# A sort that runs beside two-layer experts: one stage in place of two, the experts' pace over all of it, and the sorted keys stored by GpSimd's queue

## The reference, cut to what matters

```
src = concatenate([edge_index[0], loops]);  dst = concatenate([edge_index[1], loops])
ee    = exp(e - e_max[dst]);  alpha = ee / (segment_sum(ee, dst)[dst] + 1e-16)
agg   = segment_sum(h[src] * alpha, dst) + b_gat          # per token, 16 numbers
scores = layernorm(agg).reshape(M, HEADS, 4).mean(1)      # top 2 of 4 experts, softmax
for ei in range(4):
    hh  = gelu(x @ W1[ei] + b1[ei])                       # 128 -> 256
    out = out + g[..., None] * (hh @ W2[ei] + b2[ei])     # 256 -> 128
```

## Time and profile before

| what | us |
|---|---|
| three timed runs | 8943.16, 8943.4, 8950.78 |
| the profiled execution, its own time | 8939.67 |
| its span | 8937.9 |
| PE busy / DVE busy / ACT busy / POOL busy | 3473.0 / 3842.3 / 1988.6 / 5388.0 |
| mixer | 0 to 956 |
| words (first block of the sort) | 956 to 1043 |
| sort beside the experts | 1043 to 2043 |
| last merges, and the small part to its store | 2043 to 2155 |
| reading back of the keys, then the attention's first gathers | 2159 to 2207 |
| attention, then the weighing | 2207 to 8938 |

### The profile page before, as it was taken

The page is one execution under the profiler, slowest core; times in us unless marked ns, Lnnn a source line. Parts: engine busy times, 40 slices in busy tenths (PEclk is TensorE's granted clock), DMA queues, the critical chain, the costliest instruction groups (busy, mean ns, idle before and its releaser), DMA issues. The chain is left out here.

```text
span 8937.9 us, 45998 instructions
## 1 busy us (share of the span) xinstructions
PE 3473.0 (39%) x9579; PEld 1626.4 (18%) x9579; DVE 3842.3 (43%) x7346; ACT 1988.6 (22%) x3855; POOL 5388.0 (60%) x4840
## 2 busy tenths in 40 slices
PE   7888498991012222222222222222223222222134
PEld 4565244440000111011110110111101010100001
DVE  7888798788331212121212121212121212144498
ACT  6777255551011111111111110101010101001011
POOL 4555000001777777777777777777777777777452
PEclk8888699995555656656656656565666565656555
DMA  3343222220111111111111111111111111111166
GB/s 105 120 125 115 70 96 75 82 86 33 18 43 33 42 35 42 35 42 34 42 35 37 39 37 40 37 40 37 40 36 41 36 41 35 41 32 37 44 222 205
DMA packets 344241, 532.42 MB, mean 60 GB/s; under 512 B 159307, under 2 KB 236026, under 8 KB 319098
## 3 DMA queue, kind: packets, MB, share of 16 engines
q1 hardware_dynamic: 196514, 473.73, 15.2%
q0 software_dynamic: 147552, 56.95, 5.5%
HBM read 299.88 MB, written 230.45 MB: 59 GB/s over the span
## 5 line engine op out<-in xcount | busy, mean ns | idle before, releaser
L1136 POOL DMA_INDIRECT e_got<-rows,e_index x4352 | 4629.0, 1064 | 1456.0 <-issue 1456.0
L1594 PE MATMUL ex_y_ps<-ex_hh,w_w 128*128 128x512 f32 x1024 | 934.3, 1067 | 4143.2 <-issue 2577.9
L1629 DVE SCALAR_TENSOR_TENSOR ex_z<-ex_y_ps,w_b,ex_gate 128x512 f32<-128x512 f32 x192 | 144.1, 751 | 3256.4 <-remote 1924.9
L1594 PEld LDWEIGHTS ex_y_ps<-ex_hh,w_w 128*128 128x128 f32 x1024 | 295.9, 318 | 4624.3 <-issue 4115.9
L1612 ACT ACTIVATE ex_hh<-ex_hid_ps,w_b 128x512 f32<-128x512 f32 x512 | 322.5, 684 | 2550.3 <-remote 1756.6
L1126 POOL DMA_INDIRECT e_head<-rows,p_first x1 | 1.2, 1177 | 1194.1 <-issue 1194.1
L1576 PE MATMUL ex_hid_ps<-ex_tn,w_w 128*128 128x512 f32 x1024 | 639.6, 759 | 92.8 <-DMA ex_tn<-norm 67.9
L493 PE MATMUL o_hid_ps<-o_tn,w_w 128*128 128x512 f32 x1024 | 524.2, 594 | 72.0 <-DMA o_tn<-norm 72.0
L1232 DVE TENSOR_TENSOR_SCAN e_out<-e_near,e_out,e_wgt 128x64 f32<-128x64 f32 x1088 | 335.5, 364 | 459.5 <-issue 452.1
L506 PE MATMUL o_y_ps<-o_hh,w_w 128*128 128x512 f32 x1024 | 524.4, 594 | 14.7 <-ACT o_hh L524 14.7
L524 ACT ACTIVATE o_hh<-o_hid_ps,w_b 128x512 f32<-128x512 f32 x512 | 351.0, 687 | 364.8 <-PE o_hid_ps L493 364.8
(11 more groups left out here) (365 smaller groups left out, 6010.3 us busy)
## 6 DMA issues: line engine op xcount, KB each, us to landing
e_got<-rows,e_index POOLq DMA_INDIRECT x4352
kept<-o_kept SPq DMA_DIRECT2D x64, 1024.0 KB, 4.5
ex_gate<-gate SPq DMA_DIRECT2D x64, 1024.0 KB
c_kept<-kept SPq DMA_DIRECT2D x64, 1024.0 KB
sums<-e_out SPq DMA_DIRECT2D x68, 768.0 KB
m_xin<-in_x_dram SPq DMA_DIRECT2D x64, 512.0 KB, 4.6
mid<-m_xm SPq DMA_DIRECT2D x64, 512.0 KB, 2.9
norm<-m_tn SPq DMA_DIRECT2D x64, 512.0 KB, 4.9
```

Of the source, the lines that this page charges most:

```text
L1136: pool.indirect_dma_start(got[:, at % 2, c, :], None, rows_d, bass.IndirectOffsetOnAxis(ap=index[:, at % 2, c:c+1], axis=0)).then_inc(S["g ...
L1594: last = pe.matmul(self.y_ps[:, :], self.weights.w2[:, e, f, :], self.hh[:, e % 2 * HID + f, :], start=(f == 0), stop=(f == HID - 1))
```

## The change

`sort_keys` becomes one block. The tiles `src`, `dst`, `word` live as long as the rest of it. The last merges move into the generators `sorting()`, `copying()` and `turning()`, so they are units of the pace too: 474 units instead of 429. The experts' first five rounds (`EARLY`) are put ahead of all transposes and copies, with no pace; the other 60 rounds (480 gaps) are spread over the 474 units. The four transfers of sorted keys move from SP's queue to GpSimd's, on semaphores of their own.

```
-    STEPS, GAPS, AHEAD = EXPERTS * HID, EXPERTS * HID, 3
+    STEPS, GAPS, AHEAD, EARLY = EXPERTS * HID, EXPERTS * HID, 3, 5
...
-        UNITS = COL_BITS * (COL_BITS + 1) + PART_BITS * (1 + 2 * (PAIRS + 1) + PART_BITS - 1 + 2 * (COL_BITS - 1))
+        UNITS = (COL_BITS * (COL_BITS + 1) + PART_BITS * (1 + 2 * (PAIRS + 1) + PART_BITS - 1 + 2 * (COL_BITS - 1))
+                 + 1 + 2 * (PAIRS + 1) + 2 * (PART_BITS - 1) + 2 * (COL_BITS - 1))
...
+            yield None
+            yield from crossing(CROSS - 2)
+            for s in range(PART_BITS - 1):
+                yield None
+                yield None
+            yield from crossing(CROSS - 1)
+            for s in range(COL_BITS - 1):
+                yield None
+                yield None
...
-            sp.wait_ge(spent, 1)
-            sp.dma_start(high_flat.rearrange("(p f) -> p f", f=EDGE_COLS), upper[P - HALF // EDGE_COLS:P, :]).then_inc(stored, 16)
-            sp.wait_ge(stored, 48)
-            sp.dma_start(u_a[:, :], high_flat.rearrange("(p f) -> p f", p=P)).then_inc(u_back, 16)
-            sp.wait_ge(spent, 2)
-            sp.dma_start(low_rows, final_low[0][:, :]).then_inc(stored, 16)
-            sp.wait_ge(spent, 3)
-            sp.dma_start(high_flat.rearrange("(p f) -> p f", p=P), final_high[0][:, :]).then_inc(stored, 16)
...
+            pool.wait_ge(spent, 1)
+            pool.dma_start(high_flat.rearrange("(p f) -> p f", f=EDGE_COLS), upper[P - HALF // EDGE_COLS:P, :]).then_inc(away, 16)
+            pool.wait_ge(away, 16)
+            pool.dma_start(u_a[:, :], high_flat.rearrange("(p f) -> p f", p=P)).then_inc(u_back, 16)
+            pool.wait_ge(spent, 2)
+            pool.dma_start(low_rows, final_low[0][:, :]).then_inc(away, 16)
+            pool.wait_ge(spent, 3)
+            pool.dma_start(high_flat.rearrange("(p f) -> p f", p=P), final_high[0][:, :]).then_inc(away, 16)
+            pool.wait_ge(away, 48)
...
             if other:
-                pace = Pace(turning_on, UNITS, other.ROUNDS * other.GAPS)
-                for r in range(other.ROUNDS):
+                other.start_tensor(pe)
+                for r in range(other.EARLY):
+                    other.tensor(pe, r, lambda: None)
+                pace = Pace(turning_on, UNITS, (other.ROUNDS - other.EARLY) * other.GAPS)
+                for r in range(other.EARLY, other.ROUNDS):
                     other.tensor(pe, r, pace)
```

More of the change, by code:

```diff
@@ L539, in __call__, with sort_keys @@
             self.given += 1
-def sort_keys(nc, edges_d, keys_d, half, flag, other):
+def sort_keys(nc, edges_d, keys_d, half, flag, gathers, other):
     PAIRS, CELL, RING = 4, 512, 4
@@ L564, in halves @@
             return v[:, :, 0, :], (v[:, :, 1, ::-1] if mirrored else v[:, :, 1, :])
[L566 to L659, removed]
@@ L661, in sort_keys @@
+        src, dst, word = (sb(n, [P, EDGE_COLS], I32) for n in ("src", "dst", "word"))
+        if other: other.preparing(ctx)
         spans = []
@@ L713, in _ @@
         def _(sp):
+            sp.dma_start(src[:, :], edge_rows[0]).then_inc(loaded, 16)
+            sp.dma_start(dst[:, :], edge_rows[1]).then_inc(loaded, 16)
+            if other: other.start_sync(sp)
+            sp.wait_ge(const, 1)
+            sp.dma_start(keys_d[0:1].rearrange("(a b) -> a b", a=1), pad[0:1, 0:1]).then_inc(stored, 16)
+            sp.dma_start(keys_d[1 + EDGES + HALF:1 + EDGES + HALF + TAIL].rearrange("(a b) -> a b", a=P), pad[:, :]).then_inc(stored, 16)
             if other:
@@ new lines, in _ @@
+            v.wait_ge(loaded, 32)
+            if flag is not None:
+                go(v.tensor_reduce(top[:, :], dst[:, :], AX.X, ALU.max)); settle()
+                v.sem_inc(flagged, 1)
+            words(ping[:, :])
+            v.sem_inc(iota, 1)
+            if other: other.start_vector(v)
+            if flag is not None:
+                v.wait_ge(flagged, 2)
+                go(v.tensor_reduce(topf[:, :], turned_ps[0:1, 0, 0:P], AX.X, ALU.max)); settle()
+                go(v.tensor_scalar(flag, topf[:, :], float(HALF), None, ALU.is_ge)); settle()
@@ new lines, in _ @@
+            v.wait_ge(iota, 2)
+            if half:
+                go(v.tensor_scalar(pong[:, :], dst[:, :], HALF - 0.5, 16.0, ALU.subtract, ALU.mult))
+                go(v.tensor_scalar(src[:, :], dst[:, :], float(HALF), 2.0 * HALF - 1, ALU.add, ALU.min)); settle()
+                go(v.tensor_copy(dst[:, :], src[:, :])); settle()
+                words(upper[:, :])
+                go(v.tensor_tensor(upper[:, :], upper[:, :], pong[:, :], ALU.max)); settle()
+            else:
+                go(v.tensor_copy(src[:, :], dst[:, :])); settle()
+                words(upper[:, :])
@@ L785, in sorting @@
                         a, b = b, a
+                settle()
+                go(v.tensor_tensor(b[:, :], a[:, :], upper[:, :], ALU.min))
+                go(v.tensor_tensor(upper[:, :], a[:, :], upper[:, :], ALU.max)); settle()
+                v.sem_inc(spent, 1)
+                yield
+                a, b = b, a
+                yield from cross(a, b)
+                a, b = b, a
+                for s in range(PART_BITS - 1, 0, -1):
+                    yield from step(a, b, 1 << (s - 1))
+                    a, b = b, a
+                yield from cross(a, b)
+                a, b = b, a
+                for s in range(COL_BITS - 1, 0, -1):
+                    yield from step(a, b, 1 << (s - 1))
+                    a, b = b, a
                 final[:] = [a, b]
@@ L857, in _ @@
                 pass
-            for x in range(CROSS - 2, CROSS):
-                for c in range(CHUNK):
-                    copy(x, c)
             for x in range(2):
@@ L1862, in program @@
         with ExitStack() as c0:
-            sort_keys(nc, edges, keys[0], 0, flag[:, :], Outputs(nc, c0, weights, norm, kept, TOKEN_TILES))
+            sort_keys(nc, edges, keys[0], 0, flag[:, :], gathers, Outputs(nc, c0, weights, norm, kept, TOKEN_TILES))
         low = Places(nc, ctx, 0)
```

79 lines of the change are left out of this document (52 added, 27 removed).

## The result

The changed kernel takes 8900.1 us (median of five runs, 8889.7 to 8906.0), beside 8943.4 for the kernel before on the same chip (8940.9 to 8950.8). The ratio is 0.9947, with a 95% interval of 0.9936 to 0.9959: 43 us saved, 0.5%, and the interval leaves no change out. Forecast were 8895 and 8880 to 8912.

What follows compares the result with a forecast made beforehand. It took TensorE's expert rows between crossings as the sort's bound. 28.0 + 29.2 - 8.0 - 0.5 + 0.5 - 0.7 = 48.5 us off the median 8943.4 gave 8895, range 8880 to 8912.

Steps and rivals of the forecast that it cites:

- TensorE is the bound from crossing 0 on, at 0.858 us a row: In the sort from 1400 to 2043, VectorE waits for TensorE's expert rows: 0.858 us each, plus 5.67 us a crossing.
- The rival of no effect (ScalarE): Crossing waits come from ScalarE, not TensorE, so taking rows out brings nothing: 8943 us; chance 0.03.
- The slow rival: With experts spread thinner, the clock stays at 1.2 GHz for them too: about 9280 us; chance 0.04.
- Even crossings, 28.0 us: At crossings 2 to 12, fewer rows make VectorE the bound; its waits fall from 35.1 to 7.1 us.
- Odd crossings, 29.2 us: At crossings 1 to 13, TensorE stays the bound; 34 rows taken out gain 0.858 us each.
- The cold clock, -8.0: TensorE's new waits leave transposes cold at six even crossings, losing 1.34 us each; bounds 0 and 12.2.
- Crossings 14 and 15, -0.5: Lengths up to both unchanged; cold crossing 14 now costs 1.1 us, warm crossing 15 gives back 0.6.
- One block, 0.5: VectorE's 0.54 us wait at the end of the first block goes: 0.5 us gained.
- The early rounds cost nothing: The 80 early rows, 68.7 us, lie beside the making of words in TensorE's idle time, at no cost.
- GpSimd's stores, -0.7: Sorted-key stores after the sort: GpSimd's longer issue loses 0.7 us; lower end 0, upper end 8.
- The slow end of 8 us: Stores at the rate of GpSimd's small packets lose 8 us; part of the longer-tail rival, 8899 to 8907, chance 0.09.
- the smallest gain: Lower bound of the forecast's gain, given as 36 us: six crossings losing 2.03 each and stores at 8 us.

Runs made afterwards that it cites:

- early0: The changed kernel with no early rounds (EARLY 0), all 65 rounds of experts spread over the 474 units; 8901.8 us, ratio 0.9954.
- sortpace: The changed kernel, five early rounds kept, the other 60 spread over the sort's own 429 units, none beside the last merges; 8908.5 us, ratio 0.9961.
- light1: The changed kernel with a crossing counted as one unit of the pace instead of five (410 units) and one early round; 8856.7 us, ratio 0.9908.
- spstore: The changed kernel with the four transfers of sorted keys back on SP's queue; 8895.7 us, ratio 0.9946.
- light5: The changed kernel with a crossing counted as one unit of the pace, five early rounds kept; 8877.8 us, ratio 0.9917.
- light1sp: The changed kernel with crossings counted as one unit, one early round and the four sorted-key transfers on SP's queue; 8864.7 us, ratio 0.9905.
- poolonly: The kernel before with only the four transfers of sorted keys moved to GpSimd's queue; 8951.6 us against 8952.1, ratio 1.0001.
- actlight: The changed kernel with ScalarE's Gelu over 128 of its 512 columns, so the experts' outputs differ; one run, 8896.0 us.

## Why the prediction was right

The stretch explains the time in each kernel that was timed against the kernel before: 44.7 us in the stretch and 43 measured for the change, 44.8 and 40 for early0, 37.7 and 33 for sortpace, 86.8 and 85 for light1, 44.5 and 46 for spstore, 78.3 and 74 for light5, 87.1 and 87 for light1sp, -0.1 and 0.5 for poolonly.

- *TensorE is the bound from crossing 0 on, at 0.858 us a row.* Right: the model gives 19.72 us for crossing 2 to 3 of the changed kernel and 12.53 of light1, measured 19.73 and 12.59. The rival of no effect (ScalarE) is refuted by actlight. The slow rival is refuted by the same lengths: the rows behind cold crossings still cost 0.858 us.
- *Even crossings, 28.0 us.* The waits fell from 35.1 to 6 x 1.68 = 10.1. That is 25.1; 6 x 0.45 = 2.7 of the missing 2.9 is the cold clock's first part (a warm crossing shows 1.23 in light1), which the prediction had as a term of its own. TensorE waits 3.16 or 4.88, as worked out (3.2 to 5.0).
- *Odd crossings, 29.2 us.* The seven waits fell from 70.4 to 44.2, by 26.2; in rounds 2 to 7 each is 0.5 longer than the rows alone would give, again the clock. The first is 9.36, with 9.4 forecast; the last two are 3.88 and 4.50, with "some 4" forecast.
- *The cold clock, -8.0.* The mechanism was right and its size was off: this term is where the sum failed. I took the mean of three cold crossings, 1.34 us, but all six even crossings cost 2.0 (6.50 to 6.56 us against 4.51), 12.2 together, the upper bound that I had given. That is 4.2 us too little, and the stretch fell 4.0 short of the 48.7 that the sum had up to there. (The 5 us between 8895 and 8900 show nothing by themselves, as the runs spread over 16.4.) The waits above hold 2.7 + 3.0 of the 12.2; nearly all the rest lies inside the even crossings, where VectorE's sixteen operations take 6.42 us at crossing 2, and 5.39 in early0 with warm transposes. That is why the waits fell by 50.6 us and the stretch by only 44.7. The Trainium skill (TensorE: Matmul & The Clock Gate, HAM oscillation) says that waits between bursts throttle the clock again and each burst starts cold. The changed kernel's trace agrees for all six waits of 3.16 to 4.88 us; other runs do not for every wait, since two of 3.46 and 3.47 us in actlight left the transposes warm, at 4.56 and 4.57. So that all six cost the most was not to be had from the rows before: the term's size was open between its bounds, and it came out at one of them.
- *Crossings 14 and 15, -0.5.* From 14 to 15 it is 36.14 us instead of 34.82, and crossing 15 is warm at 4.51 instead of 5.41, which gives back 0.9 where the prediction had 0.6: 0.4 lost.
- *One block, 0.5.* The wait of the earlier trace rows is gone: the row multiplication begins at 1045.77, right behind its predecessor.
- *The early rounds cost nothing.* Right: while the words are made VectorE waits as before (for a load, 11.6 and 11.4 us, and twice for GpSimd, 11.5 and 3.2 in both kernels), and TensorE stands 71.77 us at crossing 0 ("some 70"). I did not see that they also bring nothing once the last merges take rows (early0).
- *GpSimd's stores, -0.7.* Measured 9.44 - 8.92 = 0.52 in the changed kernel, 0.75 alone. The slow end of 8 us did not come: the 2 MB went out in time. GpSimd's four issues took 0.54 to 0.78 us each, and the wait for the keys grew by no more than that. The Trainium skill (SBUF — State Buffer, SBUF: two separate sides) warns that GpSimd cannot write descriptors beside VectorE's two-port modes. No run here shows that case: the stores stand beside minima and maxima, none beside a sign multiplication, the operation that ran at double rate.

With the measured terms, the clock's part of the waits put back (25.1 + 2.7 and 26.2 + 3.0), the sum is 27.8 + 29.2 - 12.2 - 0.4 + 0.5 - 0.5 = 44.4. The stretch and its ends show nearly the same: 44.7, with 0.5 gained at the block and 0.5 lost in the tail.

Three small steps of the prediction's working do not come out as written, and none carries the forecast: the slow stores would end 2163 - 2157 = 6 us later and not 7; the smallest gain is 28.0 + 29.2 - 12.2 - 0.5 + 0.5 - 8.0 = 37.0 and not 36; and the even waits were worked out as 1.1 us each but summed with 1.2 (a warm one measured 1.23 in light1).

## What to carry to other kernels

Where one engine's work is spread over another's, count the rows ahead of each meeting point, and compare them with the time that the other engine needs up to it; a pace that weighs a step by the wrong engine's time (here a crossing as five) puts work where there is no room. Take out just so much that the engine comes in time: a wait of 2 to 5 us at a meeting point can give back, by a cold clock, what the removed rows had gained (light5 against light1), and a wait of 1.44 us cost nothing here. Two changes that each make the other engine the bound do not add up, so test each alone.

## What the hardware showed

- Whether the 32 fp32 transposes behind a wait ran cold did not go by the wait's length alone. Waits of 3.16 us in the changed kernel left them all cold (6.55 and 6.52 us), one of 2.10 in light5 slowed them to 5.55, but two of 3.46 and 3.47 in actlight left them warm (4.56 and 4.57). All six waits of 1.44 or 1.45 us in light1 left them at 4.57. In the changed kernel's wait of 4.88 us the clock was still 1.00 between 1476 and 1477 and was at 0.53 in the last microsecond of the wait.
- The price of such a cold burst varied: 6.50 to 6.56 us at the changed kernel's even crossings, 5.40 to 6.67 at light5's, 5.41 behind a wait of 119.70 us in early0 and 5.41 behind one of 5.18 in actlight. A longer wait does not make it dearer; what decides stays open.
- GpSimd issued a direct transfer of 2 MB in 0.54 us, and small ones in 0.54 to 0.78, less than the 1.06 us of its indirect one of 128 rows, by which I had priced it, and more than the 0.32 of SP.
